# A selective scan (two Mamba blocks) and two 3x3 convolutions on one core: scans written to SBUF, VectorE's products one scan later, float32r convolution parts

## The reference, cut to what matters

```python
def _mamba(x, W_in, conv_w, conv_b, W_x, W_dt, b_dt, A_log, D_skip, W_out):
    xz = einsum('bld,ed->ble', x, W_in);  xc, z = split(xz, 2)
    xc = silu(causal_conv4(xc, conv_w) + conv_b)
    dbc = einsum('ble,re->blr', xc, W_x)                 # dt (8), B (16), C (16)
    dt = softplus(einsum('blr,er->ble', dbc[..., :8], W_dt) + b_dt)
    # for each of 16 states n and 256 channels d, along the 32 steps of a sequence:
    #   h = exp(dt * A) * h + (dt * xc) * B[n] ;  y += h * C[n]
    y = (y + xc * D_skip) * silu(z)
    return einsum('ble,de->bld', y, W_out)

x1, x2 = x.reshape(b * h, w, c), x.reshape(b * w, h, c)
x = _mamba(x1, ...1) + _mamba(x2, ...2) + x              # x: (4, 128, 32, 32)
out = relu(batch_norm(x, gamma0, beta0))
out = conv3x3(out, mean|w0| * sign(w0))
out = relu(batch_norm(out, gamma1, beta1))
return conv3x3(out, mean|w1| * sign(w1)) + x
```

## Time and profile before

| what | us |
|---|---|
| median of 3 runs (lowest, highest) | 888.1 (886.25, 889.18) |
| the profiled execution's own time | 886.25 |
| its span | 884.5 |
| head, until the first scan starts | 44.4 |
| first scan's start to last scan's start | 722.5 |
| last tail of the sums, projections and statistics, to the first convolution matmul | 14.5 |
| two convolution layers and the output | 103.0 |

### The profile page before, as it was taken

How to read it: one execution, slowest core, us unless ns; L and a number is a source line. 1 busy time by engine, 2 the same in 40 slices (tenths; PEclk the granted TensorE clock), 3 DMA queues, 4 the chain that set the end, 5 groups by cost and what they waited for, 6 DMA issues and landing times.

```text
span 884.5 us, 13300 instructions
## 1 busy us (share of the span) xinstructions
PE 777.8 (88%) x4606; PEld 367.0 (41%) x4614; DVE 764.4 (86%) x504; ACT 728.2 (82%) x1305; POOL 707.7 (80%) x331
## 2 busy tenths in 40 slices
PE   5776989898999998989999989899999867689898
PEld 3433434343444443434544435354444334244343
DVE  2198999999999999999999999999999999871441
ACT  2798999999999999999999999999999995350310
POOL 0478899999999999999999999999999999300000
PEclk9888999999999999999999999999999987989999
DMA  6606152434242434443434344344444350000011
GB/s 191 253 36 241 49 182 107 177 136 185 106 176 114 167 124 154 159 156 134 151 138 146 144 130 184 126 164 128 161 122 168 113 200 1 1 1 1 0 48 48
DMA packets 39147, 110.99 MB, mean 125 GB/s; under 512 B 7244, under 2 KB 9384, under 8 KB 39080
## 3 DMA queue, kind: packets, MB, share of 16 engines
q1 hardware_dynamic: 36896, 109.81, 34.6%
q10 hardware_dynamic: 2184, 0.33, 0.2%
HBM read 106.97 MB, written 3.15 MB: 125 GB/s over the span
## 4 chain that ended last, share of the span: by engine, by line
DVE 39%; PE 21%; issue 19%; ACT 17%; POOL 2%; ACTq 0%; DMA 0%; POOLq 0%; DVEq 0%
DVE state L763 19%; DVE bank L763 15%; PE bank L1108 11%; ACT product L597 5%; ACT bank L573 4%; ACT state L584 4%; PE bank L959 3%; DVE state L773 2%; PE bank L952 2%; POOL state L511 2%; PE bank L1043 1%; PE bank L894 1%; ACT dt L627 1%; ACT L622 1%; PE bank L938 1%
## 5 line engine op out<-in xcount | busy, mean ns | idle before, releaser
L511 POOL TENSOR_TENSOR state<-state,c_wide 128x1024 f32<-128x1024 f32 x159 | 372.9, 2364 | 17.4 <-DVE state L763 17.3
L502 POOL TENSOR_TENSOR state<-u,b_wide 128x1024 f32<-128x1024 f32 x128 | 301.6, 2369 | 13.2 <-PE bank L959 7.4
L959 PE MATMUL bank<-state,ident 64*64 64x512 f32 x2048 | 260.8, 619 | 0.5 <-POOL state L511 0.5
L763 DVE TENSOR_TENSOR_SCAN state<-state,bank 128x1024 f32<-128x1024 f32 x95 | 214.8, 2271 | 0.7 <-ACT state L584 0.5
L597 ACT ACTIVATE product<-u_tok,b_tok 128x256 f32<-128x256 f32 x512 | 212.4, 497 | 2.3 <-PE bank L952 1.8
L952 PE MATMUL bank<-ident,product 128*128 128x128 f32 x1024 | 145.4, 288 | 77.1 <-ACT product L597 32.6
L952 PEld LDWEIGHTS bank<-ident,product 128*128 128x128 f32 x1024 | 117.4, 147 | 173.1 <-issue 92.7
L573 ACT ACTIVATE bank<-dt,a_neg 128x512 f32<-128x512 f32 x256 | 165.6, 677 | 26.3 <-DVE state L763 13.4
L584 ACT ACTIVATE state<-dt,a_neg 128x512 f32<-128x512 f32 x256 | 166.6, 711 | 0.2 <-PE bank L959 0.2
L763 DVE TENSOR_TENSOR_SCAN state<-bank,state 128x1024 f32<-128x1024 f32 x64 | 145.3, 2270 | 6.0 <-ACT bank L573 6.0
L763 DVE TENSOR_TENSOR_SCAN bank<-bank,state 128x1024 f32<-128x1024 f32 x64 | 146.2, 2284 | 1.1 <-ACT bank L573 0.3
(11 more groups left out here) (91 smaller groups left out, 529.1 us busy)
## 6 DMA issues: line engine op xcount, KB each, us to landing
c_wide<-bc_rows SPq DMA_DIRECT2D x128, 512.0 KB, 5.8
b_wide<-bc_rows SPq DMA_DIRECT2D x48, 512.0 KB, 7.6
b_wide<-bc_rows SPq DMA_DIRECT2D x32, 256.0 KB, 3.6
x_t<-in_x_dram SPq DMA_DIRECT2D x4, 512.0 KB, 4.9
out_dram<-x_t SPq DMA_DIRECT2D x8, 256.0 KB, 2.0
k_room<-in_L_conv_w_dram SPq DMA_DIRECT2D x2, 576.0 KB, 7.1
bc_rows<-dbc SPq DMA_DIRECT2D x16, 64.0 KB, 1.6
state<-in_L_conv_W_in_dram SPq DMA_DIRECT2D x2, 256.0 KB
```

What stands on the lines that cost most here:

```text
L502: pool.tensor_tensor(tile(n), u[:, :, :], over_halves(b_wide[:, PLAIN.index(s), :]), ALU.mult).then_inc(plain_input, 1)
L511: pool.tensor_tensor(tile(n), tile(n), over_halves(c_wide[:, n % NST, :]), ALU.mult).then_inc(output_pool, 1)
L763: dve.tensor_tensor_scan(flat(target), flat(decay), flat(source), 0.0, ALU.mult, ALU.add).then_inc(scanned, 1)
L959: return pe.matmul(y_sum[64 * h:64 * h + 64, b, :], weights[rows, :], source[rows, h, :], start=first, stop=last)
```

## The change: what it does

1. Every scan writes to `tile(n)` in SBUF, also where VectorE does the product with C. VectorE's product now reads two SBUF tiles, and it stands one scan later. A PSUM pair is free as soon as its scan is done.
2. A quarter of u (256 of 1024 columns) is made by VectorE (`make_u`), the rest by GpSimd, which waits for it.
3. The tables that set the order, the turned states and `POOL_C` are others. There are still 8 turned states and 10 products with C per item on GpSimd.
4. The head is cut into finer waits: loads have semaphores of their own, the first projection needs three groups instead of eight, ScalarE and VectorE share the copies in another way, the convolution weights are loaded after the first item's broadcasts, and GpSimd no longer waits for all groups.
5. The convolutions use two float32r parts instead of three bfloat16 ones, with padded rows of 33: 18 matmuls per tile. The sign weights are copied to float32r by GpSimd within the last item.

```diff
-PARTS = 3
+PARTS = 2
-TURNED = (1, 3, 6, 7, 10, 13, 14, 15)
+TURNED = (1, 5, 6, 9, 11, 12, 13, 15)
-POOL_C = (0, 1, 2, 3, 7, 8, 10, 12, 14, 15)
+POOL_C = (0, 1, 2, 4, 7, 9, 10, 11, 12, 15)
+U_POOL = 3 * HALVES * CHUNK // 4
...
         def wait_pair_free(eng, n):
-            last = n - PAIRS
-            if last < 0:
-                return
-            if by_pool(last):
-                wait(eng, scanned, last + 1)
-            else:
-                wait(eng, output_dve, dve_outputs(last + 1))
+            wait(eng, scanned, n - PAIRS + 1)
...
-                target = tile(n) if by_pool(n) else pair[n % PAIRS]
-                dve.tensor_tensor_scan(flat(target), flat(decay), flat(source), 0.0,
+                dve.tensor_tensor_scan(flat(tile(n)), flat(decay), flat(source), 0.0,
                                        ALU.mult, ALU.add).then_inc(scanned, 1)
...
-                dve.tensor_tensor(tile(n), pair[n % PAIRS], over_halves(c_wide[:, s, :]),
+                dve.tensor_tensor(tile(n), tile(n), over_halves(c_wide[:, s, :]),
                                   ALU.mult).then_inc(output_dve, 1)
...
-                    if k >= 0:
-                        times_c(n)
+                    times_c(n - 1)
+                    if s == DVE_U and k >= 0:
+                        make_u(k + 1)
...
+            def make_u(k):
+                wait(dve, dt_ready, HALVES * (k + 1))
+                wait(dve, xc_ready, 2 * k + 2)
+                wait(dve, u_tok_mm, 2 * k)
+                wait(dve, plain_input, before(PLAIN, NST * k))
+                dve.tensor_tensor(flat(u)[:, U_POOL:], flat(dt[k % 2])[:, U_POOL:], flat(xc[k % 2])[:, U_POOL:],
+                                  ALU.mult).then_inc(u_part, 1)
...
-                    pool.tensor_tensor(u[:, :, :], dt[m][:, :, :], xc[m][:, :, :], ALU.mult).then_inc(u_ready, 1)
+                    wait(pool, u_part, k + 1)
+                    pool.tensor_tensor(flat(u)[:, 0:U_POOL], flat(dt[m])[:, 0:U_POOL], flat(xc[m])[:, 0:U_POOL],
+                                       ALU.mult).then_inc(u_ready, 1)
...
-                    if k < 0 and NST * k + POOL_B.get(s, (0,))[0] == 0:
-                        pool.wait_ge(setup_mm, NG)
...
+            def exact_weights(n):
+                pool.wait_ge(k_copied, 4)
+                wait(pool, plain_input, before(PLAIN, LAST))
+                pool.tensor_copy(k_exact[n], k_t[n][:, :, :]).then_inc(k_exact_ready, 1)
...
-                    dve.tensor_tensor(rest, full, inner(0, n), ALU.subtract).then_inc(act_rest, 1)
-                    dve.wait_ge(act_rest, g + 1)
-                    dve.tensor_copy(inner(1, n), rest).then_inc(act_mid, 1)
-                    dve.wait_ge(act_mid, g + 1)
-                    dve.tensor_tensor(inner(2, n), rest, inner(1, n), ALU.subtract).then_inc(act_lo, 1)
+                    dve.tensor_tensor(inner(1, n).bitcast(F32R), by_row(act_f[:, n % 2, :]), inner(0, n),
+                                      ALU.subtract).then_inc(act_lo, 1)
...
-                            mm = pe.matmul(bank[n].rearrange("p (r w) -> p r w", w=W)[:, dst[0], dst[1]], k_t[layer][:, q, :],
-                                           image(part, n // 2)[:, src[0], src[1]],
+                            mm = pe.matmul(by_row(bank[n])[:, dst, :], k_exact[layer][:, q, :],
+                                           shifted(part, q)[:, src, 0:W],
```

More of the change, by code:

```diff
@@ L527, in prepare, with pads @@
                                 FAR).then_inc(dt_far, 1)
+            def exact_weights(n):
+                pool.wait_ge(k_copied, 4)
+                wait(pool, plain_input, before(PLAIN, LAST))
+                pool.tensor_copy(k_exact[n], k_t[n][:, :, :]).then_inc(k_exact_ready, 1)
+            def pads():
+                wait(pool, plain_input, before(PLAIN, LAST))
+                for s in range(COVERED):
+                    wait_output(pool, LAST - NST + s)
+                for part in range(PARTS):
+                    pool.memset(parts[part][:, 0:PART:PADDED], 0.0).then_inc(pads_ready, 1)
             for k in range(-1, ITEMS):
@@ L598, in products, with gates @@
                                    scale=b_tok[k % 2][:, blk, s:s + 1]).then_inc(product_ready, 1)
+            def gates(k):
+                wait(act, gated, HALVES * (k - 1))
+                for h in range(HALVES):
+                    wait(act, z_mm, 2 * k + h + 1)
+                    act.activation(gate[k % 2][:, h, :], z_place(k)[h], ACT.Silu).then_inc(gate_ready, 1)
             def prepare(k, s):
@@ L628, in prepare @@
                     act.preload_act_table_set("exp_and_others")
+                    if k == 0:
+                        for a in range(MAMBAS):
+                            a_log(a)
+                        for g in BY_ACT:
+                            if g in GROUPS_AT_DT:
+                                setup_copy(act, copy, g, setup_act)
                 if s == ACT_B_TOK:
@@ L880, in _, with target_half @@
         def _(pe):
+            def target_half(g):
+                return sum(GROUPS[q][:2] == GROUPS[g][:2] for q in range(g))
             def transposes(g):
                 what, which, sources, cols, _, _ = GROUPS[g]
-                last = g - SETUP_BANKS
-                if last >= 0:
-                    pe.wait_ge(setup_act if last % 2 == 0 else setup_dve, last // 2 + 1)
+                if g >= SETUP_BANKS:
+                    pe.wait_ge(*copied(g - SETUP_BANKS))
                 if what == "x":
-                    pe.wait_ge(load_x, 16 * X_LOADS[which])
-                else:
-                    pe.wait_ge(load_w[which], W_LOADS)
-                    pe.wait_ge(taps_ready, HALVES * (which + 1))
+                    pe.wait_ge(load_x[X_PIECE[which]], 16)
+                if what == "tap":
+                    pe.wait_ge(taps_ready, HALVES * which + target_half(g) + 1)
+                if what == "z":
+                    pe.wait_ge(load_taps[which], TAP_LOADS)
+                if what == "small":
+                    pe.wait_ge(load_small[which], SMALL_LOADS)
+                if what == "out":
+                    pe.wait_ge(load_out[which], OUT_LOADS)
                 for j, src in enumerate(sources):
@@ L928, in project @@
                 h, tap = part // KCONV, part % KCONV
+                if k == 1 and tap == 0:
+                    pe.wait_ge(*copied((8, 9)[h]))
                 if part == 0:
@@ L1072, in _ @@
                         sum_states(NST * k + e)
[L1073 to L1075 removed]
+                    if k < 0:
+                        for slot, groups in ((PE_DBC, GROUPS_AT_DBC), (PE_DT, GROUPS_AT_DT),
+                                             (PE_B_TOK, GROUPS_AT_B_TOK), (PE_U_TOK[1], GROUPS_AT_U_TOK)):
+                            if s == slot:
+                                for g in groups:
+                                    transposes(g)
                     if image_output(k) is not None:
```

391 lines of the change are left out of this document (226 added, 165 removed).

## The result

The changed kernel takes 945.1 us (median of 4 runs, 940.2 to 945.7) against 888.4 for the kernel before on the same chip: the ratio is 1.063, 95% interval 1.059 to 1.067. Slower, as forecast, and within the range; the forecast was 950.

The account below looks back on a forecast made before the run. VectorE and GpSimd were both taken as full, with GpSimd the bound after the change through a shared SBUF read path. 886.25 - 10 (head) + 104 (middle stage) - 30 (convolutions) = 950 us, 8-in-10 range 905 to 1015.

Parts of the forecast that it names:

- The bound and the item: Middle stage: VectorE and GpSimd both full, 44.1 and 44.4 us of work per item, against 44.23 measured.
- stalls of the first two items: Middle stage of the kernel before: the 15 us left beyond 16 items of 44.23 us, which make 707.7.
- Two operands in SBUF: Middle stage: VectorE's two-SBUF-input instructions and GpSimd share a read path; item 51.4 us, +115, less 11 at the ends: +104.
- VectorE's part of u: Each item: a quarter of u costs VectorE 0.34 us and saves GpSimd 0.55; alone, the stage gains 8 us.
- rival (a): Middle stage: no shared path, L749 was late for another reason; total 838 us, faster than before; chance 0.09.
- The PSUM pair: Middle stage: TensorE's 24.2 us of waits for VectorE to free a pair go, but TensorE has slack; counted 0.
- Head: Before the first scan: finer waits let the projection and GpSimd's work start earlier; -10 us, bounds -4 to -15.
- Tail: From last scan to first convolution matmul: no change forecast, 0 us.
- Convolutions: Convolution tiles: 18 matmuls instead of 27, 3.82 us per tile instead of 5.72; -30 us over 16 tiles.
- one-pass price: Convolutions: a float32r matmul needs one column pass and costs the bfloat16 pace, 0.212 us.
- rival (b): Shared path, with float32r convolution matmuls at the pace of one float32 record, 0.43 us; total 1012 us; chance 0.10.

Follow-up runs that it names:

- memset kernels: Changed kernel with VectorE's products with C replaced by memsets, 862.0 us; the same under the old orders with u whole on GpSimd, 853.8 us.
- pair of memset kernels: Changed kernel with VectorE's products with C as memsets: 862.0 us with VectorE's quarter of u, 858.5 us with u whole on GpSimd.
- undoing experiment: Changed kernel with VectorE's own scans writing to PSUM again and its product right behind its scan, reading PSUM: 938.7 us, ratio 1.054.
- the fastest kernel: Kernel before with only the new head and float32r convolutions; old tables, products from PSUM, u whole on GpSimd: 859.4 us, ratio 0.965.
- kernel with 64 weight columns: Changed kernel with 64 instead of 128 columns of weights in each convolution matmul, half of the output channels left out: 939.8 us in one run.
- a plain run: Changed kernel with the convolutions' moving operand read as one run of 512 or 480 columns instead of padded rows: 939.3 us in one run.

## Why the prediction was right

**The bound and the item.** Right. The sum of start-to-start times gave 44.1 for VectorE and 44.4 for GpSimd, so that any lengthening of either would show. The 44.23 is a short item, though (the mean is 44.5), so that some 4 of the 15 us put down to "stalls of the first two items" are in all the others.

**Two operands in SBUF.** Right in its mechanism, and it rested on one instruction of 0.80 us in the trace of before. It was forecast that GpSimd becomes the bound and that the item is 51.4; it did, and the item is 50.34. The forecast wait of 0.1 to 0.4 us per product of VectorE is right as a mean (0.4) and not as a picture: 59 of the 97 wait less than 0.15, and 21 wait 1.2 to 1.7. The memset kernels make the cause shown: 82 and 83 us of the middle stage go when VectorE's products no longer read, under two sets of orders. The Trainium skill's rule ("SBUF — State Buffer", "Who interferes with whom") held in both directions, and also where it excludes a GpSimd instruction that only writes. That the second one waits until the first is done is too little in one place: with GpSimd's products in a gapless row VectorE's waited for five of them (11.48 us). The size of the term was a little high. 93 of VectorE's 97 products hold one of GpSimd's, six per item, for 0.98 us on average instead of 1.14; VectorE's part of u holds none (0.34 counted), because GpSimd waits for it anyway, idle for 0.73 where it was 0.17. So 43.7 + 6 x 0.98 + 0.56 = 50.1, against 50.34 measured and 51.4 forecast. Over 16 items that is 17 of the 20 us by which the middle stage fell short.

**VectorE's part of u.** The price was right (0.43, and 1.81 instead of 2.36 on GpSimd), the effect was not. The step that failed is "u loses a quarter, 0.6 us: 44.23 - 0.55 = 43.7 us": the edit adds a wait on each side, and I named neither what stands behind `make_u` in VectorE's queue nor GpSimd's idle time until it is done. The pair of memset kernels puts it at a loss of 3.0 us in the middle stage, where I had counted the 8 us as a gain; beside the shared path it is neither (945.2 and 945.1). So rival (a) was priced too low: without the path the changed kernel would not take 838 but 862.

**The PSUM pair.** "I count 0" fits the changed kernel, where GpSimd is the bound, and it hid a dependence: the waits of the undoing experiment point to new orders that need the early pair.

**Head.** -4.4 instead of -10. The loads landed earlier, as assumed (the scaling started at 4.15 instead of 6.95), but the projection began at 8.82, not near 6.5, and dt was ready at 25.8, not near 22. What failed besides is GpSimd's start near 25. It stood idle until VectorE's part of u, which came at 29.28: in VectorE's queue it stood behind three copies and four small scalings (all from 25.67 on). GpSimd's part and its first product followed:

```profile
4.15 1.29 DVE L797 TENSOR_TENSOR state<-state,conv_w 128x512 f32<-128x512 f32 x2 [2.73 <-DMA state<-in_L_conv_W_in_dram]
...
29.28 0.42 DVE L829 TENSOR_TENSOR u<-dt,xc 128x256 f32<-128x256 f32 x1
...
29.88 1.81 POOL L586 TENSOR_TENSOR u<-dt,xc 128x768 f32<-128x768 f32 x1 [26.96 <-DVE u L829]
...
31.84 9.31 POOL L563 TENSOR_TENSOR state<-u,wide 128x1024 f32<-128x1024 f32 x4
```

With u whole on GpSimd (the fastest kernel) its products began at 27.32, but the first scan came at 40.65 all the same. The trace shows one reason: the small scalings ahead of it in VectorE's queue, which read a single tile, were held too. The four took 6.7 us, and three of them ended within 0.05 us of one of GpSimd's products each (29.70 and 29.66, 32.04 and 32.00, 34.35 and 34.30):

```profile
27.76 2.02 DVE L809 TENSOR_SCALAR a_neg<-a_neg 128x32 f32<-128x32 f32 x2
29.70 4.65 DVE L817 TENSOR_SCALAR d_diag<-ident,vectors 128x64 f32<-128x64 f32 x2
```

```profile
27.32 6.99 POOL L569 TENSOR_TENSOR state<-u,wide 128x1024 f32<-128x1024 f32 x3
```

In the changed kernel, with GpSimd idle, the same four took 0.26 and 0.41 us by pairs. The memset kernel with u on GpSimd has the same held scalings, and its first scan comes at 41.7 where the one with the quarter on VectorE has 39.8. How much of the head they cost, no run tells.

**Tail.** +3.9 where I had 0. Two products instead of one stand behind the last scan, but that is the smaller part. The kernel with 64 weight columns has the same list of instructions up to the convolutions, and its tail is 15.1 us, 0.6 above the 14.5 of before. What differs is the time of the same matmuls, the sums (L1071) and the output projection (L1163). First the changed kernel, then the other:

```profile
850.33 3.69 PE L1071 MATMUL bank<-state,ident 64*64 64x512 f32 x16 [2.23 <-DVE state L886]
855.52 5.84 PE L1163 MATMUL bank<-w_out,k_room 128*128 128x128 f32 x32 [1.50 <-DVE k_room L898]
```

```profile
849.04 2.23 PE L1071 MATMUL bank<-state,ident 64*64 64x512 f32 x16 [1.95 <-DVE state L886]
852.77 4.01 PE L1163 MATMUL bank<-w_out,k_room 128*128 128x128 f32 x32 [1.50 <-DVE k_room L898]
```

Their granted clock was 0.50 and 0.65 in the first, and 1.00 for both in the second. So 3.3 of the 3.9 us came with the clock of the profiled execution. The head differs between the two executions as well: the same eight matmuls of the first projection took 5.83 us here and 3.71 there (records 0.85 us apart at first, against 0.43), though the profile shows a granted clock of 1.00 for both, and the first scan started at 40.0 and 38.1. Together that is the 5 us between 945 and the 940 of the kernels with 64 columns and with a plain run. The changed kernel's own fastest run has 940.2 too, but no profile.

**Convolutions.** The one-pass price was right in kind: 4.19 us per tile, 0.233 per matmul, against 0.212 forecast and 0.43 in rival (b). The gain was 25.5 instead of 30. What the Trainium skill says of 4-byte data read and cut, beside four passes for true float32 ("FP8 and Floating Point Precision", "TensorE Precision Notes"), agrees to within that 10%.

The errors of head, tail and convolutions (+5.6, +3.9, +4.5) and that of the middle stage (-19.7) have opposite signs; the 950 came closer to the 944.6 of the profiled run than its terms did, and that much of it is luck.

## What to carry to other kernels

Before moving an operand from PSUM to SBUF, ask which of VectorE's instructions then read SBUF twice, and whether GpSimd reads SBUF beside them: if both engines are full, each such pair costs about a VectorE instruction on GpSimd's side and a wait on VectorE's. Look for one small instruction of that kind in the trace you have; its length is a hint, and a run has to confirm it. To price a contention, replace the instruction by one of the same length that doesn't take part and leave every wait alone; undoing the edit measures the orders as well. Splitting a product between two engines was no relief here, where the split adds a handover in each round. And before a difference of a few us is put down to the code, compare the same instructions in another execution, with the granted clock beside them.

## What the runs showed of the hardware

- A VectorE product with two SBUF inputs and a GpSimd product exclude each other for whole instructions: 1.19 us became up to 2.90, 2.36 became up to 3.37, both in the changed kernel. A GpSimd memset doesn't take part (0.94 to 0.97 us beside such products), nor does a VectorE memset (0.91 us in all of 97, and no product of GpSimd above 2.41).
- The two need not alternate: in the kernel before with scans to SBUF, two of VectorE's products stood behind a gapless row of GpSimd's products and took 11.5 us.
- A GpSimd product that is held is longer by 0.98 us on average, less than the 1.14 for which VectorE's product takes its engine.
- Small VectorE scalings of one tile in SBUF (128 x 32 and 128 x 64 float32; the latter by a column of scalars) were held as well: 6.7 us for four beside GpSimd's products, 0.67 with GpSimd idle.
- Among 512-column matmuls the distance from start to start is 0.238 us for float32r, in one record, 0.216 for bfloat16, and 0.86 for float32, in two records.
- The same sixteen sums took 3.69 us at a granted clock of 0.50 and 2.23 at 1.00.
- A VectorE memset of 128 x 1024 float32 takes 0.91 us, a GpSimd one 0.95.
